# Two schedules in a fused attention and feed-forward kernel: when the first block splits the expert weights, and which engine writes the routing's token numbers

## The reference, cut to what matters

```python
x = x + L0_xattn(layernorm(x), ctx)       # latent attention, 16 heads
x = x + L0_ffn(layernorm(x))              # ternary weights, silu(gate) * up, rms norm, down
x = x + L1_xattn(layernorm(x), ctx)       # causal attention
x = x + L1_ffn(layernorm(x))              # 32 experts, 8 of them for each token
...
def _L0_ffn_ref(x, w_gate_up, w_proj):    # 512 -> 2 x 2048 -> 512
    gate, up = jnp.split(jnp.einsum('bsd,hd->bsh', x, wq_gu), 2, axis=-1)
    hn = rms_norm(jax.nn.silu(gate) * up)
    return jnp.einsum('bsh,dh->bsd', hn, wq_p)
...
def _L1_ffn_ref(...):
    topv, topi = jax.lax.top_k(probs, TOP_K)
    combine = combine.at[jnp.arange(T)[:, None], topi].add(routing_weights)
    # each expert: h @ w_d.T * c_e over the tokens that chose it
```

## Time and profile before

| | us |
|---|---|
| median of 3 runs | 1912.48 |
| lowest and highest run | 1911.66, 2383.33 |
| the profiled execution, its own time | 1905.04 |
| the span of its trace | 1903.2 |

### The profile page before, as it was taken

How to read it: one execution, slowest core, us unless ns; L and a number is a source line. 1 busy time by engine, 2 the same in 40 slices (tenths; PEclk the granted TensorE clock), 3 DMA queues, 4 the chain that set the end, 5 groups by cost and what they waited for, 6 DMA issues and landing times. The chain is left out here.

```text
span 1903.2 us, 36290 instructions
## 1 busy us (share of the span) xinstructions
PE 1626.2 (85%) x12199; PEld 1038.3 (55%) x12199; DVE 1215.5 (64%) x2716; ACT 1065.8 (56%) x2664; POOL 641.4 (34%) x478
## 2 busy tenths in 40 slices
PE   5868998999999889898988887655489999999993
PEld 4645756656656645555544455443356666666662
DVE  4556797796796797696787667766733333333332
ACT  2436855855846736575675776642745555555552
POOL 3452503503503400000000123221057777777772
PEclk9679999999999999999998899776589999999997
DMA  6850130120120039696777001011436565566536
GB/s 192 255 173 1 31 95 18 34 86 15 34 87 15 32 104 335 223 318 213 229 240 253 33 2 36 28 34 48 117 81 138 125 157 135 136 135 149 130 77 218
DMA packets 143366, 226.62 MB, mean 119 GB/s; under 512 B 37887, under 2 KB 93439, under 8 KB 143062
## 3 DMA queue, kind: packets, MB, share of 16 engines
q1 hardware_dynamic: 113846, 203.01, 33.6%
q0 software_dynamic: 29344, 21.29, 6.9%
HBM read 175.00 MB, written 98.80 MB: 144 GB/s over the span
## 5 line engine op out<-in xcount | busy, mean ns | idle before, releaser
L2698 PE MATMUL g_ps<-ring,xT 128*128 x1572 | 299.5, 326 | 1.0 <-issue 1.0
L996 POOL TENSOR_TENSOR pr<-pr,sm 100x1444 f32<-100x1444 f32 x64 | 166.2, 2597 | 362.1 <-DVE sm L1028 362.1
L2647 POOL DMA_INDIRECT acc<-rows,slot_sources x131 | 207.8, 1586 | 105.1 <-issue 61.0
L2804 DVE SCALAR_TENSOR_TENSOR hf<-sg,g_ps 128x192 f32<-128x192 f32 x131 | 46.4, 354 | 236.1 <-ACT sg L2753 236.1
L2698 PEld LDWEIGHTS g_ps<-ring,xT 128*128 128x128 f16 x1572 | 141.8, 98 | 71.7 <-issue 5.9
L2637 POOL DMA_INDIRECT xg<-xtab,slot_sources x131 | 137.9, 1052 | 87.6 <-issue 85.5
L1023 DVE TENSOR_REDUCE sm<-s_banks 100x2 f32<-100x722 f32 x128 | 115.8, 905 | 76.5 <-PE s_banks L767 75.9
L2720 PE MATMUL d_ps<-ring,hT 128*128 x655 | 162.8, 379 | 0.7 <-ACT hT L2766 0.7
L920 ACT ACTIVATE pr<-s_banks,sm 100x361 f32<-100x361 f32 x256 | 142.1, 567 | 33.8 <-DVE sm L1023 29.8
L767 PE MATMUL s_banks<-kvp,qp 128*100 128x361 f16 x768 | 139.6, 319 | 8.6 <-ACT pr L920 4.2
L824 PE MATMUL o_bank<-cT,N_hi 128*128 128x400 f16 x512 | 129.6, 335 | 0.0
(11 more groups left out here) (325 smaller groups left out, 3917.8 us busy)
## 6 DMA issues: line engine op xcount, KB each, us to landing
split_f<-in_gu SPq DMA_DIRECT2D x64, 384.0 KB, 4.5
split_gu<-split_o SPq DMA_DIRECT2D x64, 384.0 KB, 3.3
ring<-split_gu SPq DMA_DIRECT2D x32, 768.0 KB
head<-in_head SPq DMA_DIRECT2D x16, 864.0 KB, 6.5
tern_w<-in_tern SPq DMA_DIRECT2D x48, 256.0 KB, 3.2
split_f<-in_down SPq DMA_DIRECT2D x32, 384.0 KB, 4.1
split_d<-split_o SPq DMA_DIRECT2D x32, 384.0 KB, 3.5
ring<-split_d SPq DMA_DIRECT2D x32, 256.0 KB
```

Of the source, the lines that this page charges most:

```text
L996: nc.gpsimd.tensor_tensor(pr[:, s % 3], pr[:, s % 3], small[:, s % 3, 2, :].unsqueeze(2).to_broadcast([SEQ, 4, KEYS]), ALU.mult).then_inc( ...
L2647: nc.gpsimd.indirect_dma_start(out=core.acc[i % NACC][:, :], out_offset=bass.IndirectOffsetOnAxis(ap=core.sources[:, i:i + 1], axis=0), in ...
L2698: last = nc.tensor.matmul(g_ps[i % 2][:, 0:2 * INTER], xT[:, i % 2, a * KT + k, :], ring(i, (2 * k + w) * 2 * INTER, 2 * INTER), start=((k ...
```

## The change

In ffn0 `STEP_SPLITS` takes the place of "piece t in step t": steps 0 to 3 split pieces 0 to 3, step 4 pieces 4 and 5, step t from 5 to 14 piece t + 1, step 15 pieces 16 and 17. `LATE_SPLITS` gives two pieces to each of down blocks 0 to 2 (18 and 19, 20 and 21, 22 and 23). In route the batches 3, 7, 11 and 15 (`compared`) are done without `tile_hot` and without ScalarE: VectorE writes `tile_token` by eight `tensor_scalar` instructions of 131 elements, each comparing an iota with one choice's tile number and multiplying by the token's number. GpSimd makes the iota for it, one small instruction more.

```diff
-LATE_SPLITS = (range(HT, HT + 3), range(HT + 3, HT + 6), range(HT + 6, HT + 8), ())
+STEP_SPLITS = [range(t + (t > 4), t + (t > 4) + 1 + (t in (4, HT - 1))) for t in range(HT)]
+LATE_SPLITS = [range(HT + 2 + 2 * m, HT + 4 + 2 * m) for m in range(KT - 1)] + [()]
...
                         if t < HT:
-                            es.hi(act, c, t)
+                            for j in STEP_SPLITS[t]:
+                                es.hi(act, c, j)
...
                             low(c, t - 1)
-                            es.lo(dve, c, t - 1)
+                            for j in STEP_SPLITS[t - 1]:
+                                es.lo(dve, c, j)
                             add_square(c, t - 1)
...
+    def compared(b):
+        return b % OH == OH - 1
+    def turn_of(b):
+        return b // OH if compared(b) else b // OH * (OH - 1) + b % OH
+    def id_ready(engine, b):
+        steps = id_made if compared(b) else tile_id
+        engine.wait_ge(steps.sem, steps.after(turn_of(b)))
...
                     pe.wait_ge(rank_hot.sem, rank_hot.after(b))
-                    pe.wait_ge(tile_id.sem, tile_id.after(b))
+                    id_ready(pe, b)
...
-                    act.wait_ge(tile_hot.sem, tile_hot.after(b))
+                    if compared(b):
+                        continue
+                    act.wait_ge(tile_hot.sem, tile_hot.after(turn_of(b)))
...
-                    if b >= OH:
-                        dve.wait_ge(tile_id.sem, tile_id.after(b - OH))
-                    one_hot(hot_q[:, b % OH], TILES, q16[:, b, :]).then_inc(tile_hot.sem, 1)
+                    if b >= OH and compared(b):
+                        dve.wait_ge(hot_used.sem, hot_used.after(b - OH))
+                    elif b >= OH:
+                        id_ready(dve, b - OH)
+                    if compared(b):
+                        for k in range(TOPK):
+                            nc.vector.tensor_scalar(hot_id[:, b % OH, k, :], iota_h[:, :], q[:, b, k:k + 1],
+                                                    token[:, b:b + 1], ALU.is_equal, ALU.mult).then_inc(id_made.sem, 1)
+                    else:
+                        one_hot(hot_q[:, b % OH], TILES, q16[:, b, :]).then_inc(tile_hot.sem, 1)
```

More of the change, by code:

```diff
@@ L2336, in route @@
     rank_hot, tile_hot, tile_id, hot_used = (Steps(core, n) for n in ("rank_hot", "tile_hot", "tile_id", "hot_used"))
+    id_made = Steps(core, "tile_id_made", per=TOPK)
+    def compared(b):
[5 more added lines that the diff above has]
+        engine.wait_ge(steps.sem, steps.after(turn_of(b)))
     consts = core.sem("route_consts")
@@ L2367, in route @@
         iota8 = core.sb(ctx, "iota_eight", [SEQ, TILES, TOPK], F16)
+        iota_h = core.sb(ctx, "iota_h", [SEQ, TILES], F16)
         listf = core.sb(ctx, "slots_f", [P, TILES], F32)
@@ L2464, in _ @@
                 const(nc.gpsimd.tensor_copy(iota8[:, :, :], tile_of[0:SEQ, :].unsqueeze(2).to_broadcast([SEQ, TILES, TOPK])))
+                const(nc.gpsimd.tensor_copy(iota_h[:, :], tile_of[0:SEQ, :]))
                 const(nc.gpsimd.memset(tiles[:, :, :], 0.0))
@@ L2558, in _ @@
                 ts(core.sources[:, 0:TILES], listf[:, :], -1.0, None, ALU.add)
-ROUTE_CONSTS = 9
+ROUTE_CONSTS = 10
 TRI_MADE = 3
```

## The result

The median of 20 runs with the change is 1907.02 us (1899.58 to 1910.86). The kernel before has 1917.57 over the 20 runs that stand beside them, of which the one of 2383.33 is left out of the ratio. The ratio is 0.9945, with a 95% interval of 0.9932 to 0.9958: about 10.5 us less (8 to 13), where 16.5 were forecast. The kernel before was itself 5.1 us longer in this comparison than the 1912.48 that the forecast started from; in the later comparisons its median was 1911.1 to 1912.7 again. The profiled execution took 1902.05 us, its span is 1900.2.

What follows compares the result with a forecast made beforehand. No engine's total bounds the kernel: ffn0 loses time to late weight pieces, route is bound by ScalarE. Savings of 11.0 us in ffn0 and 5.5 in route, 16.5 together, took 1912.5 to 1896.0 us; range 1886 to 1907.

Steps and rivals of the forecast that it cites:

- ffn0, what is removed: Late copies of the down block's sums, `add_rows` waits and slow clock behind them vanish at chunk joints: 19.3 us saved.
- Step 4: ffn0, chunks 1 to 3: the second piece delays ScalarE by 0.84 and VectorE by 0.93, 1.77 us each, 5.3 us added.
- Step 15: ffn0, end of steps: VectorE's longer last loop delays `hT_lo` and the last chunk's square sums, 0.8 us in four chunks, 3.2 added.
- Loads in steps 4 to 8: ffn0: pieces wanted one step earlier mostly land just in time; 0 to 1.5 us added, 0.5 taken.
- the rival on the other side: ffn0: loads come late in steps 4 to 8, about 20 places over four chunks; time up to 1938 us, chance 0.04.
- The end of the stage: End of ffn0: the last store sets the next stage's start; only VectorE's 0.7 us wait gained, 3.1 if TensorE set it.
- route: ScalarE bounds it; four fewer instructions there, less a new wait and other costs, save 5.5 us, between 0.3 and 7.0.

## Why the prediction missed

The time lies 0.02 us above the range, with the right sign, and 11.0 above the 1896.0 of the forecast. Of these 5.1 are the base: the kernel before had 1917.57 in this comparison and not 1912.48, and from 1917.57 the same forecast gives 1901.1. Why it was longer there stays open. The other 6.0 are the gain, 10.5 us where 16.5 were forecast, and they lie in ffn0: that half alone gained 4.1 (1 to 6) where 11.0 were forecast. By its steps:

- **ffn0, what is removed: right.** Forecast 19.3 us at the joints; 3.9 us in step 0 and 1.2 of slow clock in step 1, three times, with the 4.4 for `add_rows` make 19.7.
- **Step 4: right.** Forecast 1.77 us a chunk. Chunk 2's steps take 43.91 us, 0.79 more than before, although 1.2 us of slow clock have gone from them: 2.0. Beside the 42.1 of a chunk without a doubled step it is 1.8.
- **Step 15: the term was mis-sized.** Its 0.8 us came (1.62 to 2.42). It took the price of a wait to be the wait, though the prediction had itself counted the slow clock behind a wait of 3.40 us. Here the price is 1.7 to 3.5 us on top wherever the clock falls, 2.7 in the mean. Before, two waits of 1.62 us carried it in 8 of 20 cases like them, 0.8 blocks a run; after, two of 2.42 (9 of 10) and one of 1.62 in chunk 0 make 2.2 blocks: 1.4 more by 2.7 is 3.8 us. The last chunk's block, behind 1.85 us for the square sums where it was 1.01, adds 3 of 4 cases by 1.7, so 1.3. That is an estimate of 5.1 us, wide by the few cases.
- **Loads in steps 4 to 8: the second mis-sized term.** Forecast 0.5 with 1.5 as the end, measured 3.8, all of it in chunk 1. The step that failed is that the pieces would land just in time in that chunk too. The argument went from the landing times of single pieces, and of the 3.3 MB beside them it said only that a mean rate leaves room. A mean says nothing of the piece that is issued behind 1.8 MB in one lump. It was the mechanism of the rival on the other side, in one place instead of 20. Moving the two transfers took away 2.7 of it. The row of 830.88 above, in the trace that the prediction read, was the warning; the prediction looked at the chunks without these transfers.
- **The end of the stage: 0.7 forecast, nothing came.** VectorE:

```profile
1033.95 1.13 DVE L1491 SCALAR_TENSOR_TENSOR x_rows<-row_ps,rms,x_rows 100x128 f32<-100x128 f32 x4 [2.58 <-PE row_ps L1349]
1035.00 1.96 DVE L1182 SCALAR_TENSOR_TENSOR split_o<-split_f,split_o 128x384 f16<-128x384 f32 x4
```

  The last low parts stood behind ScalarE's late piece before; now they stand behind `add_rows`, which waits for TensorE. They end at 1036.96 instead of 1036.90, and the next stage begins 3.4 us later (3.25 before). TensorE is done 1.5 us earlier than before and nothing follows from it, which fits the reading that the last store sets the end.
- **route: right, but something is given back behind it.** Forecast 5.5, measured 5.9 for the stage. The comparisons take 0.224 us, inside the bounds of 0.10 and 0.48 and under the 0.26 that I took; the wait is 1.43 instead of 1.75. The Trainium skill, "VectorE: DVE Perf Modes", gave estimates of 0.095 us by its formula and 0.19 with its measured fixed part (the section on the TRN2 errata); this case is longer than both, and nearer to the second. The prediction's 0.278 us, of another form, was half as long again as that 0.19, so "agrees" said too much. Behind the list the experts' first 12 matmuls run partly at half clock (3.75 us, and 2.57 before; 4.02 in the profile of the pieces' schedule alone, with the old routing):

```profile
1386.72 3.75 PE L2725 MATMUL g_ps<-ring,xT 128*128 x12
```

  The fourth `hf` comes 23.1 to 23.5 us after the list in all 10 profiles with the new routing, 22.1 in two of three with the old one and 23.7 in the third. That is probably 1 us of the gain; the third profile forbids to call it shown. With it route is worth 4.8, and the run of that half alone had 4.5.

The terms that were off sum to 5.1 + 3.3 + 0.7 + 1.1 = 10.2 us, less 0.4 each by which the joints and route did better, 9.4; the miss of the gain is 6.0, with an interval of some 2.5 to either side, so the sum explains about 1 us too much even at its edge. The half clock's term is the soft one. The range missed by the two together, the base and the gain. Its spread was taken around one profile that had none of these blocks slow, and no row of that profile could show how often they are; 20 runs of the kernel before, of 1910 to 1926, would have shown that the base was uncertain.

From the experts' fourth `hf` to their last the profile of after takes 466.1 us, 2.3 more than that of before (463.8). In the other 11 profiles it is 463.9 to 464.6, nine of them with the new routing, so that is no effect of the change.

## What to carry to other kernels

Price a wait of the busiest engine in two parts, the wait and the clock behind it, and when an edit lengthens a wait, count the second part by how often the profiles show it behind waits of that length; one profile is not enough for that. When work is moved earlier in a stage that streams its input, go through the other transfers of the same queue by name and place, and look for waits that cost nothing yet; a mean rate says nothing about the piece that stands behind the large one. And where an execution is profiled once, compare its time with the fastest and the median run before adding to it (this one was the lucky case), and give the base a spread of its own.

## What the chip showed that I had not expected

TensorE fell to its lower level of 1.2 GHz after short waits between stretches in which it was hardly ever idle. A part of the 32 matmuls of 400 columns ran at it (0.54 us instead of 0.33 for one), mostly with the four `ln_ps` and the eight `row_ps` ahead of them, and the block took 6.9 to 8.5 us instead of 5.57. The same wait of 1.62 us, at the same place of the same program, led to it in one profile twice and in the other not at all, which accounts for 6.6 of the 9 us between their ffn0. The Trainium skill, "TensorE: Matmul & The Clock Gate", Part 1, says that the number of slow matmuls at a kernel's start varies from run to run. These profiles were not read at the start; in the middle of the kernel they show the same, 0 or 2 slow blocks behind the same waits. A wait of 3.52 us in the steps of the second chunk also ended in nine slow matmuls, but only 1.2 us after the matmuls had begun again (the kernel with steps 8 and 11 doubled):

```profile
833.01 0.34 PE L1319 MATMUL gate_ps<-hT_hi,wt 128*128 128x400 f16 x1 [3.52 <-DVE hf L1449]
...
834.04 0.38 PE L1319 MATMUL gate_ps<-hT_hi,wt 128*128 128x400 f16 x1
834.21 0.54 PE L1319 MATMUL gate_ps<-hT_lo,wt 128*128 128x400 f16 x1
```
